# Four edits around the dense layer of a four-layer convolution kernel: who adds the last half block, when its statistics are joined, which taps are turned first, and where two early loads stand in the queue

## The reference, cut to what matters

```
x = x + depthwise(_gn(x), w1, b1, w2, b2)     # layer 0
x = x + dense(_gn(x), W)                      # layer 1: sign(x) and sign(W), 3 x 3, 32 x 32 channels
x = x + depthwise(_gn(x), ...)                # layer 2
x = x + depthwise(_gn(x), ...)                # layer 3

def depthwise(x, w1, b1, w2, b2):             # its taps are computed from x itself
    pooled  = x.mean(axis=(2, 3))
    hdn     = relu(pooled @ w1 + b1)
    kernels = (hdn @ w2 + b2).reshape(b, 32, 3, 3)
    return conv of each channel with its own 3 x 3 taps, zero padding
```

## Time and profile before

| | |
|---|---|
| median of 3 runs | 4339.41 us (4338.14 to 4343.95) |
| the profiled execution | 4362.16 us, its span 4360.3 us |
| PE busy | 3266.8 us, 75% of the span |
| DVE busy | 2071.6 us, 48% |
| ACT busy | 1784.8 us, 41% |
| POOL busy | 1956.4 us, 45% |
| mean granted clock of TensorE | 0.898 of full speed |
| chain that ended last, by engine | PE 42%, DMA 24%, SP's queue 11%, DVE 8%, ACT 5% |

### The profile page before, as it was taken

How to read it: one execution, slowest core, us unless ns; L and a number is a source line. 1 busy time by engine, 2 the same in 40 slices (tenths; PEclk the granted TensorE clock), 3 DMA queues, 4 the chain that set the end, 5 groups by cost and what they waited for, 6 DMA issues and landing times.

```text
span 4360.3 us, 70554 instructions
## 1 busy us (share of the span) xinstructions
PE 3266.8 (75%) x26592; PEld 2091.4 (48%) x26592; DVE 2071.6 (48%) x6038; ACT 1784.8 (41%) x2626; POOL 1956.4 (45%) x3175
## 2 busy tenths in 40 slices
PE   0676987769876787777886787866877769777698
PEld 0443545435454454544455454553545536445355
DVE  2627643266432754337543384424744257432573
ACT  2443633336343463435434354343542436424232
POOL 1326544265433654346442564326543265332754
PEclk9988998889988898888988899988999889888899
DMA  6388697876969669596786967869778697786946
GB/s 210 58 149 169 147 318 198 155 163 153 337 166 176 163 184 327 130 213 143 198 299 123 212 153 219 288 106 211 148 227 280 105 209 159 236 268 106 205 79 218
DMA packets 589273, 829.51 MB, mean 190 GB/s; under 512 B 489731, under 2 KB 490502, under 8 KB 572550
## 3 DMA queue, kind: packets, MB, share of 16 engines
q1 hardware_dynamic: 323200, 734.28, 66.4%
q10 hardware_dynamic: 216582, 76.68, 8.2%
q0 software_dynamic: 49152, 14.05, 2.1%
HBM read 375.89 MB, written 267.45 MB: 148 GB/s over the span
## 4 chain that ended last, share of the span: by engine, by line
PE 42%; DMA 24%; SPq 11%; DVE 8%; ACT 5%; ACTq 4%; POOL 4%; issue 3%; DVEq 0%; POOLq 0%
PE acc L979 24%; PE acc L996 12%; SPq L327 9%; DMA arena<-x 6%; DMA out<-y 6%; DMA dense_out<-arena 5%; POOL y L510 3%; DMA arena<-signs 3%; PE acc L1058 3%; ACT arena L599 2%; ACTq L606 2%; DMA signs<-arena 2%; ACTq L535 2%; DVE dense_stats L860 1%; DMA arena<-y 1%
## 5 line engine op out<-in xcount | busy, mean ns | idle before, releaser
L979 PE MATMUL acc<-y,arena 64*128 64x384 f32 x9216 | 1726.5, 501 | 179.9 <-ACT y L568 146.1
L979 PEld LDWEIGHTS acc<-y,arena 64*128 64x128 f32 x9216 | 1014.0, 194 | 739.2 <-ACT y L568 230.6
L327 POOL DMA_DIRECT2D arena<-y x1536 | 790.6, 522 | 836.7 <-PE acc L996 725.4
L996 PE MATMUL acc<-arena 64*128 64x384 f32 x4608 | 958.4, 509 | 226.3 <-issue 208.9
L568 ACT ACTIVATE y<-acc 128x768 f32<-128x768 f32 x832 | 644.4, 808 | 1177.0 <-PE acc L996 1176.1
L489 POOL TENSOR_SCALAR arena<-arena,cst,fill 128x24 f32<-128x24 f32 (+1 forms) x1536 | 613.7, 419 | 710.7 <-issue 469.8
L510 POOL TENSOR_TENSOR y<-arena,y 128x3072 f32<-128x3072 f16 x88 | 529.9, 6045 | 735.0 <-DMA arena<-dense_out 734.9
L860 DVE BATCH_NORM_STATS2 dense_stats<-y 128x6 f32<-128x192 f32 x1536 | 408.0, 344 | 729.2 <-POOL y L510 728.9
L996 PEld LDWEIGHTS acc<-arena 64*128 64x128 f32 x4608 | 525.1, 196 | 450.7 <-issue 240.9
L1058 PE MATMUL acc<-arena,wd_side 128*32 128x384 fp8e4 (+1 forms) x10752 | 471.8, 330 | 287.1 <-DMA arena<-signs 234.6
L802 DVE TENSOR_SCALAR_CACHE_REDUCE y<-acc 128x768 f32<-128x768 f32 x256 | 245.1, 958 | 640.3 <-PE acc L996 640.3
(11 more groups left out here) (86 smaller groups left out, 1287.1 us busy)
## 6 DMA issues: line engine op xcount, KB each, us to landing
y<-x SPq DMA_DIRECT2D x64, 2304.0 KB, 27.1
out<-y SPq DMA_DIRECT2D x64, 2304.0 KB, 22.9
arena<-y SPq DMA_DIRECT2D x768, 141.0 KB
arena<-x SPq DMA_DIRECT2D x168, 576.0 KB, 6.5
dense_out<-arena ACTq DMA_DIRECT2D x384, 192.0 KB, 7.0
arena<-dense_out SPq DMA_DIRECT2D x192, 384.0 KB, 7.0
arena<-y SPq DMA_DIRECT2D x768, 71.9 KB
arena<-signs SPq DMA_DIRECT2D x192, 250.0 KB, 10.3
```

Of the source, the lines that this page charges most:

```text
L327: eng.dma_start(halo[at:at + n, slot, :, d0:d0 + size], y[source:source + (n - 1) * step + 1:step, first + odd:first + odd + 3:2, s0:s0 + ...
L979: nc.tensor.matmul(acc[:, 2 * k + odd, 0:KN], w_center[at, slot, 2 * q + odd, :], y[at, 2 * g + odd, k * KN:(k + 1) * KN], start=turn == 0 ...
L996: nc.tensor.matmul(acc[:, 2 * k + odd, 0:KN], w_halo[at, slot, q, :], halo[at, bt % HALO_SLOTS, q, k * KN:(k + 1) * KN], start=False, stop ...
```

## The change

There are four edits.

1. The last of the 12 blocks of the dense result is split: VectorE adds its first 8 channels, POOL the other 8.
2. The statistics of the first five windows are joined before that addition (`add_blocks` with 10 parts of equal size); after the last blocks only three parts per channel are joined, with weights.
3. At the start of a depthwise stage TensorE makes the taps of channels 0 and 1 by a product of their own (18 columns, `ps_first`), and VectorE makes the weights of pair 0 from them, then halo taps and weights of batch 0, then pair 1, then all the rest (`first_weights`). Small results are laid out anew over the banks of PSUM, so that `group_variances` no longer waits for `fill_ready` in the second and third stage.
4. In the queue of SP the first two early loads stand behind the halo copies of batch 0, ahead of those of batches 1 and 2.

```
+        ps_gmean = [acc[:, k, o:o + C] for k, o in ((7, FREE), (5, 0), (5, 0))]
+        ps_half = [acc[:, k, o:o + C] for k, o in ((7, FREE + C), (5, C), (5, C))]
+        ps_var = [acc[:, k, o:o + C] for k, o in ((7, FREE + 2 * C), (4, 0), (4, 0))]
...
-                for b in range(HALO_SLOTS):
-                    halos(first + b)
+                halos(first)
                 for i in range(AHEAD_SLOTS):
                     load_ahead(s, i)
+                for b in range(1, HALO_SLOTS):
+                    halos(first + b)
...
+                        for n in range(WINDOWS * D_HALVES):
                             w, half = n // D_HALVES, n % D_HALVES
                             uses = s * (WINDOWS * D_HALVES // D_SLOTS) + n // D_SLOTS + 1
                             pool.wait_ge(d_loaded[n % D_SLOTS], 16 * 2 * uses)
-                            at = y[:, half * D_CH:(half + 1) * D_CH, w * WN:(w + 1) * WN]
-                            nc.gpsimd.tensor_tensor(at, d_in[:, n % D_SLOTS], at, ALU.add).then_inc(d_added, 1)
+                            first = D_SHARED if n == WINDOWS * D_HALVES - 1 else 0
+                            at = y[:, half * D_CH + first:(half + 1) * D_CH, w * WN:(w + 1) * WN]
+                            nc.gpsimd.tensor_tensor(at, d_in[:, n % D_SLOTS, first:], at, ALU.add).then_inc(d_added, 1)
...
+            def pair_centers(d, g):
+                if d > 0:
+                    dve.wait_ge(acc_full[THIRDS - 1], 2 * (d * BATCHES - 1) * BATCH_PAIRS)
+                at = slice(2 * g, 2 * g + 2)
+                by_row("c", turned_c[:, at], spread_c[:, at], 2)
+                by_column("c", spread_c[:, at], w_center[:, 0, at], 2).then_inc(center_ready, 1)
...
-            def first_centers(d):
-                dve.wait_ge(taps_ready, d + 1)
-                turn_centers(slice(0, BATCH_CH))
-                center_weights(d, 0, BATCH_PAIRS)
...
-            def first_halos():
+            def turn_halos(pairs):
...
+                turn("h", halo_taps[:, pairs], turned_h[:, pairs], n)
+            def first_weights(d):
+                dve.wait_ge(first_taps_ready, d + 1)
+                turn_centers(slice(0, 2), ps_first.rearrange("p (c t) -> p c t", t=TAPS))
+                pair_centers(d, 0)
+                dve.wait_ge(taps_ready, d + 1)
+                turn_halos(slice(0, BATCH_PAIRS))
                 halo_weights(0)
-                turn_centers(slice(BATCH_CH, C))
+                turn_centers(slice(2, BATCH_CH), by_tap[:, 2:BATCH_CH])
+                pair_centers(d, 1)
+                turn_centers(slice(BATCH_CH, C), by_tap[:, BATCH_CH:C])
+                turn_halos(slice(BATCH_PAIRS, PAIRS))
...
+            def add_blocks(to, blocks, counts):
+                means, spreads = blocks[:, :, :, 1], blocks[:, :, :, 2]
+                n = means.shape[2]
+                whole = sum(counts)
+                mean, spread_of = to
+                if len(set(counts)) == 1:
+                    link(nc.vector.tensor_reduce(mean, means, AX.X, ALU.add))
+                    link(nc.vector.tensor_scalar(mean, mean, 1.0 / n, None, ALU.mult))
+                    link(nc.vector.tensor_tensor(means, means, mean.unsqueeze(2).to_broadcast([P, C, n]), ALU.subtract))
+                    link(nc.vector.scalar_tensor_tensor(means, means, float(counts[0]), means, ALU.mult, ALU.mult))
+                else:
+                    weights = dense_stats[:, :, 0, 0:n]
+                    part = dense_stats[:, :, 1, 0:n]
+                    link(nc.vector.tensor_tensor(part, means, weights, ALU.mult))
+                    link(nc.vector.tensor_reduce(mean, part, AX.X, ALU.add))
+                    link(nc.vector.tensor_scalar(mean, mean, 1.0 / whole, None, ALU.mult))
+                    link(nc.vector.tensor_tensor(means, means, mean.unsqueeze(2).to_broadcast([P, C, n]), ALU.subtract))
+                    link(nc.vector.tensor_tensor(part, means, weights, ALU.mult))
+                    link(nc.vector.tensor_tensor(means, means, part, ALU.mult))
+                link(nc.vector.tensor_tensor(spreads, spreads, means, ALU.add))
+                link(nc.vector.tensor_reduce(spread_of, spreads, AX.X, ALU.add))
             def dense(s):
-                adds = WINDOWS * D_HALVES - 1
+                adds = WINDOWS * D_HALVES
                 for w in range(WINDOWS - 1):
                     for half in range(D_HALVES):
                         dve.wait_ge(d_added, s * adds + w * D_HALVES + half + 1)
-                        window_stats(w, half)
+                        last = window_stats(w, half)
+                link(last)
+                rows = dense_stats[:].rearrange("p c w s -> p c (w s)")
+                early = rows[:, :, 0:6 * (WINDOWS - 1)].rearrange("p c (b k) -> p c b k", k=3)
+                end = rows[:, :, 6 * (WINDOWS - 1) - 3:].rearrange("p c (b k) -> p c b k", k=3)
+                add_blocks((agg[:, :, 0], agg[:, :, 1]), early, [WN // 2] * (2 * (WINDOWS - 1)))
+                link(nc.vector.tensor_copy(end[:, :, 0, 1], agg[:, :, 0]))
+                link(nc.vector.tensor_copy(end[:, :, 0, 2], agg[:, :, 1]))
+                nc.vector.memset(dense_stats[:, :, 0, 0:1], float((WINDOWS - 1) * WN))
+                link(nc.vector.memset(dense_stats[:, :, 0, 1:3], float(WN // 2)))
                 w, n = WINDOWS - 1, WINDOWS * D_HALVES - 1
                 dve.wait_ge(d_loaded[n % D_SLOTS], 16 * 2 * (s + 1) * (WINDOWS * D_HALVES // D_SLOTS))
-                nc.vector.memset(acc[:, 7, C * TAPS:C * TAPS + (BATCH_CH + BATCH_PAIRS) * 4 * R], 0.0)
-                at = y[:, D_CH:C, w * WN:(w + 1) * WN]
-                nc.vector.tensor_tensor(at, d_in[:, n % D_SLOTS], at, ALU.add).then_inc(d_added_last, 1)
+                nc.vector.memset(spread_all, 0.0)
+                at = y[:, D_CH:D_CH + D_SHARED, w * WN:(w + 1) * WN]
+                nc.vector.tensor_tensor(at, d_in[:, n % D_SLOTS, 0:D_SHARED], at, ALU.add).then_inc(d_added_last, 1)
+                dve.wait_ge(d_added, (s + 1) * adds - 1)
+                window_stats(w, 0)
                 dve.wait_ge(d_added_last, s + 1)
-                window_stats(w, 1)
                 dve.wait_ge(d_added, (s + 1) * adds)
-                link(window_stats(w, 0))
-                of = dense_stats[:].rearrange("p c w (e k) -> p c (w e) k", k=3)
-                means, spreads = of[:, :, :, 1], of[:, :, :, 2]
-                mean, spread_of = agg[:, :, 0], agg[:, :, 1]
-                link(nc.vector.tensor_reduce(mean, means, AX.X, ALU.add))
-                link(nc.vector.tensor_scalar(mean, mean, 1.0 / (2 * WINDOWS), None, ALU.mult))
-                link(nc.vector.tensor_tensor(means, means, mean.unsqueeze(2).to_broadcast([P, C, 2 * WINDOWS]),
-                                             ALU.subtract))
-                link(nc.vector.scalar_tensor_tensor(means, means, float(WN // 2), means, ALU.mult, ALU.mult))
-                link(nc.vector.tensor_tensor(spreads, spreads, means, ALU.add))
-                link(nc.vector.tensor_reduce(spread_of, spreads, AX.X, ALU.add))
+                link(window_stats(w, 1))
+                add_blocks((agg[:, :, 0], agg[:, :, 1]), end, [(WINDOWS - 1) * WN, WN // 2, WN // 2])
                 dve.sem_inc(dve_stat, C)
...
             def group_variances(d):
                 pe.wait_ge(spread_ready, d + 1)
-                pe.wait_ge(fill_ready, d + 1)
-                group_sums(ps_var, spread[:]).then_inc(group_var_ready, 1)
+                if d % ND == 0:
+                    pe.wait_ge(fill_ready, d + 1)
+                group_sums(ps_var[d % ND], spread[:]).then_inc(group_var_ready, 1)
...
+                sel = cst[:, C_SEL + li * P:C_SEL + (li + 1) * P]
+                if li == 0:
+                    pe.wait_ge(hidden_ready, d + 1)
+                nc.tensor.matmul(ps_first, sel, b2_sb[:, 0:2 * TAPS], start=True, stop=False)
+                nc.tensor.matmul(ps_taps, sel, b2_sb[:], start=True, stop=False)
+                if li > 0:
+                    pe.wait_ge(hidden_ready, d + 1)
+                nc.tensor.matmul(ps_first, hidden[:], w2_sb[:, li, 0:2 * TAPS], start=False, stop=True)\
+                    .then_inc(first_taps_ready, 1)
                 nc.tensor.matmul(ps_taps, hidden[:], w2_sb[:, li, :], start=False, stop=True).then_inc(taps_ready, 1)
```

More of the change, by code:

```diff
@@ L70 @@
 D_CH = C // D_HALVES
+D_SHARED = D_CH // 2
 A_HALO = 0
@@ L502, in _ @@
                 for li in range(ND):
-                    first = (s * ND + li) * BATCHES
+                    batch = (s * ND + li) * BATCHES
                     if li == 1:
-                        for n in range(WINDOWS * D_HALVES - 1):
+                        for n in range(WINDOWS * D_HALVES):
                             w, half = n // D_HALVES, n % D_HALVES
@@ L520, in _ @@
                         if b + HALO_SLOTS < BATCHES or follows:
-                            corners(first + b + HALO_SLOTS)
```

(12 more changed lines are left out.)

75 lines of the change are left out of this document (34 added, 41 removed).

## The result

| | before | changed |
|---|---|---|
| median of 5 runs | 4339.41 us (4322.56 to 4345.68) | 4373.31 us (4368.95 to 4386.69) |
| ratio | | 1.0085 [1.006, 1.0109] |

The changed kernel is slower by 33.9 us, and the interval of the ratio lies clear of 1. The forecast was 4366, slower, with a range of 4338 to 4390. One execution of best2 (4787.87 us, granted clock 0.708) and one of the kernel before (14976.83 us) are slow ones and are left out of all medians. The first view is the head of the changed kernel's page: busy time, share of the span and number of instructions.

A forecast was written before the change was run, and what follows sets the result against it. No engine was full; the chain that ended last changed hands, so the forecast counted TensorE's waits. 11 + 15 + 8 + 5.5 - 16 + 5 - 1.5 = +27 on 4339.4 gave 4366 us, range 4338 to 4390.

The forecast's parts named there:

- The early join is held by POOL: End of dense stage: POOL's additions block VectorE's early join, so the joins end 3.5 us later a sample.
- the join isn't held up: Rival, end of dense stage: small join instructions slip past POOL's additions, 26 us off, 4340 us; chance 0.15.
- The chain: Dense stage's end to first taps: no wait for `fill` and a shorter product bring the first taps 0.97 us earlier.
- The weights ahead of pair 1 in the second stage: Start of second stage: the new weight order lets TensorE reach pair 1 1.1 us sooner after the first taps.
- The third stage's eviction: Third stage, pair 1: VectorE reaches pair 0's eviction 2.85 us later; +15 us over eight samples, +8 for slow restarts.
- the third stage takes the delay up: Rival: the third stage's later waits for early loads and stores swallow the delay, 23 us off, 4343 us; chance 0.08.
- Sample 0's first stage: First stage of sample 0: the later eviction, two more products and a slow restart cost 5.5 us.
- The early loads: Second stage, pair 2: loads issued earlier end TensorE's waits for ScalarE and three slow restarts, 16 us off.
- the border: Second stage, batch 1: halo copies behind the two loads delay POOL's border; waits and one slow restart cost 5 us.
- the two loads hold back the halo copies: Rival, second stage: early loads delay batch 1's halo copies, 32 us more, 4398 us; chance 0.11.
- -1.5: Second stage: fewer gaps in TensorE's chain may spare some slow products, 1.5 us off, called a guess.
- a steadier clock or an unseen gain: Rival: TensorE's chain gains more than seen, above all by a steadier clock, below 4330 us; chance 0.12.

The follow-up runs named there:

- best2: Changed kernel with one late join instead of the early join, and ScalarE evicting part 0 of the third stage's pairs 0 and 1: 4266.76 us, ratio 0.9823.
- b_again: The kernel before, unchanged, run once more for a second profile: 4337.15 us, ratio 1.0001.
- u_dense: Changed kernel with the split of the last block and the early join both undone: 4347.65 us, ratio 1.0022.
- u_split: Changed kernel with the last block whole on VectorE, the early join kept: 4357.95 us, ratio 1.004.
- u_join: Changed kernel with one late join instead of the early join, the last block still split: 4337.38 us, ratio 0.9996.
- u_weights: Changed kernel with VectorE's order of the first weights as before, TensorE's separate first-taps product kept: 4350.09 us, ratio 1.0029.
- evict_act: Changed kernel with ScalarE instead of VectorE evicting part 0 of pairs 0 and 1 of the third stage: 4292.58 us, ratio 0.9896.
- loads_only: Kernel before with only the two early loads moved ahead of the halo copies of batches 1 and 2: 4330.33 us, ratio 0.9973.

## Why the prediction was right

The direction, the two places of the loss and their mechanisms were right. Some terms had the wrong size, and their errors partly cancelled. The changed profile is 36.3 us longer than b_again and 11.1 longer than the first profile of before. Part by part, with the steps of the forecast's sum:

- **The early join is held by POOL** (forecast +3.5 a sample): +3.8 by the first profile, 3.7 between the changed kernel and u_dense, 3.4 by b_again. The size was right, a detail not. I let one of the two-input instructions slip in between POOL's blocks and L892 be held. In the trace the multiplication of 32 elements ahead of them (L890) is held until block 10 ends (it ends 0.04 us after it in all eight samples), and L891 is the one held by the half block, 3.46; L892 takes 0.62. The rival "the join isn't held up" is refuted by u_split and the changed kernel together: 0.62 and 3.46 for one instruction, without and with POOL beside it. (The bound named with this rival, 1.1 us, comes out as 1.0 from its own terms.) The Trainium skill (SBUF — State Buffer, "Who interferes with whom") lets two-input instructions and the two-port forms of tensor_scalar contend, and says that the order of issue decides who blocks; the trace agrees with the first for 320 elements, is consistent with the second for L890 (1.07 there against 0.18 for its twin L898), and agrees with the third in u_join, where POOL pays.
- **The chain** (-0.97): -1.33 from deviations to first taps against the first profile, -1.82 against b_again; in the third stage -1.0 and -0.8. In the second stage before, this stretch is not one value but 5.2 to 7.1 us, and 4.2 to 5.3 in the changed kernel. **The weights ahead of pair 1 in the second stage** (-1.1): -1.35, from 9.67 to 8.32 after the first taps. Forecast together +1.4 a sample at that place; measured +1.1 against the first profile, but only +0.2 against b_again. From the early statistics to the first taps the forecast has 2.5 a sample, 20 in eight; it is 20 against the first profile and 13 against b_again.
- **The third stage's eviction** (+2.85 for VectorE, +15 in all, and +8 for slow restarts): +2.90, from 12.56 to 15.46 after the first taps; the wait went from 2.16 to 6.9. The terms that the forecast shows for this wait (2.16, 2.85 and 1.1) make 6.1, not its 6.8; pair 0 gained more than 1.1 there, since its own wait for halo weights had been 1.35 in the third stage. The restart costs 2.6 as a mean, in all eight samples, where I took 2.0. Pair 2 comes 4.0 us later after the first taps than in b_again, 32 in eight. The forecast for the same stretch is 31: its 15 and 8, without the 0.97 a sample of the chain, which lies ahead of the first taps. u_weights shows that VectorE's order is the cause, evict_act that the wait and its restart are what the time hangs on. These two refute the rival "the third stage takes the delay up": they took 23 and 81 us off the whole.
- **Sample 0's first stage** (+5.5): the last early statistics of sample 0 end at 392.25, before at 385.93 and 385.15, +6.3 and +7.1. The other kernels with the new order of weights have 389.1 to 392.8.
- **The early loads** (-16) and **the border** (+5) were both mis-sized, and their sum was right by luck: it is -11, and loads_only measures -10. The +5 is not seen. The border of batch 1 starts 24.8 to 28.5 us after the half addition, not 28 to 33; the mean is 27.0, against 27.0 and 25.8 in the two profiles of before. (The first of them has 25.8 to 30.0, where the prediction read 25.5 to 29.7.) I found no wait for it, so the rival by which the two loads hold back the halo copies is out too. The -16 was read from one profile: its 11.2 us at pair 2 are 2.4 in b_again, with no slow restart behind them. And the forecast did not see that edits 1 to 3 would make these waits longer without edit 4, which holds back 45 us in the changed kernel; the sum needed no term for that.

The forecast came out 7 us low. From the first taps of the second stage to those of the third it has -29 in eight samples (1.1 and 0.97 a sample, -16, +5 and -1.5), and against b_again there are -18; against the first profile the same stretch gives -43, so that this term depends on the run of before more than on anything in the change. The other stretches add up to 54 against the forecast's 57: 13 for 20 up to the first taps, 32 for 31 in the third stage, 7 for 5.5 in sample 0, and 2 elsewhere. So the forecast was 11 too hopeful in one stretch and 7 too gloomy in another, and that the total is so near is partly chance.

The rival with the opposite sign, a steadier clock or an unseen gain, did not come: the granted clock is 0.891 over the span, 0.898 before. Left open: what in edits 1 to 3 makes edit 4 worth 45 us instead of 10, and whether edit 1 gains anything in best2.

## What to carry to other kernels

Work that is pulled forward into a wait is free only if nothing else owns the resource it needs there: look up what the neighbour engine does at that moment. Where VectorE and POOL must meet, put VectorE's instruction on the critical path first, so that it is already waiting when POOL's next one comes; in u_join POOL was then the one to lose time. A reordering that helps the first user of a list can be paid at a second place that shares the code; walk through every stage that calls it, to the first instruction behind the list. When TensorE waits for one short eviction at the end of a long list on one engine, try to give the eviction to another engine before touching the list: in the changed kernel that was worth 81 us, the reordering itself -23.

## What the runs showed of the hardware that I had not expected

- A VectorE multiplication of 128x32 elements by a constant, with one input and in place, took 1.53 us as a mean of eight beside POOL's addition, and 0.18 in the late join without it; in all eight samples it ended 0.04 us after POOL's block:

```profile
L891 DVE TENSOR_TENSOR dense_stats<-dense_stats,agg 128x320 f32<-128x320 f32 x8 | 27.7, 3466 | 0.3
...
L890 DVE TENSOR_SCALAR agg<-agg 128x32 f32<-128x32 f32 x8 | 12.2, 1525 | 0.3
...
L898 DVE TENSOR_SCALAR agg<-agg 128x32 f32<-128x32 f32 x8 | 1.5, 182 | 0.3
```

  (VectorE's groups by form in the changed kernel: count, then busy us, mean ns, idle before.) The reduction just ahead of it, with 320 elements in, took its usual 0.62.
- Between two back-to-back additions of POOL a waiting VectorE instruction gets in, a long one too: beside the half addition of u_join POOL's half block is recorded with 4.63 us, 1.52 more than in the changed kernel.
- A wait of 2.2 us of TensorE was followed by a slow restart in five of eight samples of the first profile of before and in seven of eight in b_again, at 1.7 us each; one of 6.9 us in all eight, at 2.6 us each (6.08 as a mean for 3.50, from 5.08 to 6.49).
